# A decoder layer on one core: the order of the work rewritten on all five engines

## The chip, the core and the metric

The kernel runs on one core of one Trainium2 chip. A core has five engines, each with a queue of its own which it works off strictly in order: TensorE (PE; its weight loads are PEld), VectorE (DVE), ScalarE (ACT), GpSimd (POOL) and SyncE (SP), which here only issues transfers. Engines wait for one another through semaphores. The metric is the device time of one execution in microseconds (us), as the median of several runs.

## The reference

x is 16 batches of 128 tokens of 256 values, float32. Three sublayers, each behind a layer norm without weights and added to x:

```python
x = x + attn(norm(x))   # 16 heads over 72 shared latent values, causal softmax
x = x + birwkv(norm(x), ctx, ctx, w, u)
x = x + moe(norm(x))    # 8 experts, top-2 gates, silu(x Wg) * (x Wu) Wd
# attn:   kv = xn @ latent_w + b;  q_h = xn @ Wd_w[h] + b_h
#         y_h = softmax(causal(q_h kv^T / 4)) kv;  out = concat(y_h) @ out_w
# birwkv: ek = exp(ctx); forward and backward scans with decay exp(w) of
#         ek*ctx and of ek; sum of both over sum of both, times sigmoid(xn)
```

## The kernel before

Every piece of work is a step with a name and numbers. `STEPS` (line 109) is one list of all steps, from which the counts are made that semaphores are waited for. What an engine really does in which order stands in a table of its own: `SYNC_STEPS` (198), `TENSOR_STEPS` (210), `VECTOR_STEPS` (232), `SCALAR_STEPS` (261) and `GPSIMD_STEPS` (284). The same name in two tables is the part that each engine has in it. An engine stops at the first step whose wait isn't met, and all behind it stops with it.

The batches stand in four groups of four (g) and eight pairs (k). The steps that matter here:

- Loads, on SyncE: `xl.g` x of group g, `ctx.g` its context (512 KB each), `ow` the output weights (1152 KB), `owh` the same weights by head for the last batch (also 1152 KB), `out.g.*` and `xd.g.*` stores of x and of the normalised x, `lw.j.k` and `ltk.j` weights and token lists of expert tile j.
- Norms: `bn`, `agg` (DVE), `rs` (POOL), `nmb` (DVE), `xn` (ACT), `tx` transposes (PE, then ACT and DVE copy).
- Attention: `q.k.i` is part i of five of the queries of pair k: PE multiplies, ACT copies with bias (line 1142), SyncE moves it by head (lines 713 and 717). There are 64 units n of four heads of one batch: `S.n` scores (PE, line 905), row maxima (DVE, 1373), exponentials (ACT, 1148), `N.n` reciprocal (DVE) and weighing (POOL, 1779), `T.n` transpose (PE, 913) and copy (ACT, 1153), `Y.n` times the values (PE, 923), copy (DVE, 1389) and, for a pair of batches together, packing by three transfers (SyncE, 730 and 731). The copy `Y.n` reuses one of two buffers and waits until the packing of an earlier unit has landed. `O.b.i` is a quarter of the output product of batch b (PE, 946), `xb.i` the bias (POOL, 1786), `add.i` the sum (DVE, 1396).
- Context: `w1` to `w8`, `wa`, `wb` by group and half: `w1` is ek (ACT, 1161) and ek times context (DVE, 1403), `w2` to `w5` are the scans (DVE, 1413 and 1415), `w6`, `w7`, `wa` sums on POOL, `w8` reciprocals (DVE, 1420). The first `w1` also waits for the decay table which POOL builds (line 1762 to 1768).
- Experts: 23 tiles j; the first 16 have 256 rows, the last seven 128. `lxg.j` gathers rows (POOL, 1836; two instructions for a large tile), `tg.j` transposes them, `sw.j.k` splits weights in two (ACT 1213, DVE 1299), `up`, `si`, `hd`, `sh` the hidden layer, `dn.j` the second product (PE) and its weighing into one of two buffers Y (ACT, 1242), `ao.j` adds them to the output by an accumulating indirect transfer (POOL, 1872; two instructions for a large tile). `ao.j` waits until `ao.j-1` has landed, unless both tiles are of one expert, and weighing j waits until `ao.j-2` has landed.

The wait of `ao.j`, in code:

```python
if j > PHASES[0]:
    owed = e.value_load(turns[...], ...)      # 16 or 32 if same expert
    e.wait_ge(s_acc[1 - j % 2], 16 * parts_alike(j - 1) + owed)
elif j:
    po.wait_ge(s_acc[1 - j % 2], 16 * parts_alike(j + 1))
```

Of the kernel before, what the change touches and what calls it, by code (L numbers as in the profile page):

```python
# [96 lines left out]
def gathered(j):  # L97
# [105 lines left out]
    lw.2.2 out.3.0.2 lw.3.1 ltk.4 xd.3.0.2 xd.3.2.2 lw.3.0 out.3.2.2 lw.4.0 lw.4.1 lw.5.1 lw.5.0 ltk.5 lw.6.1 ltk.6 ltk.7 lw.3.2 lw.4.2 ltk.8 ltk.9  # L203
    ltk.10 ltk.11 lw.6.0 ltk.12 lw.7.0 lw.7.1 ltk.13 ltk.14 lw.5.2 ltk.15 ltk.16 lw.8.0 lw.8.1 lw.9.0 lw.9.1 lw.6.2 lw.7.2 lw.10.0 lw.10.1 lw.11.0
    lw.11.1 lw.8.2 lw.9.2 lw.10.2 ltk.17 lw.12.0 ltk.18 ltk.19 ltk.20 lw.13.0 lw.12.1 lw.13.1 ltk.21 lw.14.0 ltk.22 lw.11.2 lw.15.0 lw.14.1 lw.12.2
    lw.13.2 lw.15.1 lw.17.0 lw.14.2 lw.16.0 lw.15.2 lw.17.1 lw.16.1 lw.16.2 lw.18.1 lw.18.0 lw.17.2 lw.19.1 lw.19.0 lw.20.0 lw.21.0 lw.20.1 lw.18.2
# [6 lines left out]
    T.7 Y.6 S.11 S.12 O.0.0 O.0.1 Y.7 T.8 q.2.4 Y.8 O.0.2 T.9 S.13 T.10 Y.9 q.3.0 T.11 va.1 Y.10 O.0.3 S.14 T.12 S.15 O.1.0 O.1.1 O.1.2 q.3.1 Y.11
    wb.0.1 q.3.2 S.16 S.17 T.13 Y.12 T.14 q.3.3 Y.13 wb.1.0 S.18 S.19 O.1.3 T.15 T.16 Y.14 O.2.0 O.2.1 q.3.4 tx.1.2.0.4.0 Y.15 T.17 S.20 S.21
    tx.1.2.0.4.1 O.2.2 Y.16 T.18 O.2.3 Y.17 S.22 S.23 O.3.0 O.3.1 T.19 O.3.2 O.3.3 q.4.0 S.24 kt.2 q.4.1 Y.18 T.20 Y.19 q.4.2 T.21 Y.20 q.4.3 T.22
    S.25 S.26 q.4.4 O.4.0 Y.21 T.23 wb.1.1 O.4.1 Y.22 T.24 S.27 S.28 T.25 Y.23 O.4.2 va.2 Y.24 S.29 S.30 q.5.0 T.26 Y.25 T.27 O.4.3 wb.2.0 Y.26 S.31
# [1754 lines left out]
```

## Time and profile before

| | |
|---|---|
| median of 3 runs | 547.34 us (546.92 to 547.79) |
| profiled execution, its own time | 550.32 us |
| its span, first to last instruction | 548.7 us |
| busy share of the span | PE 91%, PEld 80%, DVE 68%, ACT 61%, POOL 57% |
| mean granted TensorE clock | 0.965 |
| moved by DMA | 76.86 MB, 140 GB/s |

The span is 1.6 us shorter than that execution's own time, which in turn is 3.0 us above the median. Times in the rows are counted from the span's start. A busy time is what the profile has recorded of the instructions; idle time before an instruction is put down to whatever released it. An engine's share over the whole span hides that stages differ: start-up, attention (up to about 300 us), the hand-over to the experts (to about 392 us), the experts, and the end.

### The profile page before, as it was taken

To read this page: it belongs to the slowest core of one execution; us is meant where nothing else is said; L and a number is where in the kernel's file an instruction comes from. 1 tells how busy PE (TensorE), PEld (TensorE's weight loads), DVE (VectorE), ACT (ScalarE), POOL (GpSimd) and SP (SyncE) were. 2 spreads that over 40 slices of the span, in tenths; PEclk is the share of its full clock that TensorE was granted. 3 is DMA by queue.
4 is the path that set the end of the run, shared out by engine and by line. 5 is a ranking of instruction groups with operands and counts; after the bars stand their busy time and mean duration, and the time that the engine had idled before them with its cause. 6 is when DMAs were issued, how large, how long until landed. Compare 5 with 4: busy or idle time off the path is not lost.

```text
span 548.7 us, 10874 instructions
## 1 busy us (share of the span) xinstructions
...
## 2 busy tenths in 40 slices
...
GB/s 233 168 125 100 26 108 117 37 22 163 49 110 95 49 40 55 132 52 67 68 139 44 146 209 214 260 84 215 214 235 244 208 234 237 247 258 276 310 11 0
DMA packets 48087, 76.86 MB, mean 140 GB/s; under 512 B 11053, under 2 KB 29742, under 8 KB 47830
## 3 DMA queue, kind: packets, MB, share of 16 engines
...
## 4 chain that ended last, share of the span: by engine, by line
PE 45%; DVE 16%; issue 12%; DMA 10%; POOL 7%; ACT 4%; POOLq 2%; SPq 1%; another core or an unknown queue 1%; ACTq 0%; DVEq 0%
PE P L830 14%; DMA out<-Y,TK 10%; PE P L905 7%; PE P L923 7%; PE PO L946 7%; PE P L913 4%; PE PO L830 3%; POOL cxa L1836 3%; DVE EB L1373 2%; POOL out L1872 2%; DVE arena L1413 2%; DVE arena L1415 1%; PE P L856 1%; DVE ZT L1389 1%; DVE WF L1299 1%
## 5 line engine op out<-in xcount | busy, mean ns | idle before, releaser
L1779 POOL TENSOR_TENSOR EB<-EB,small 128x512 f32<-128x512 f32 x64 | 72.1, 1138 | 72.9 <-DVE small L1378 72.8
L1148 ACT ACTIVATE EB<-EB,small 128x128 f32<-128x128 f32 x256 | 99.1, 394 | 14.5 <-DVE small L1373 14.5
L830 PE MATMUL P<-GT,WF 128*128 128x256 f32 x768 | 100.4, 291 | 4.2 <-DVE HF L1646 2.0
L1872 POOL DMA_INDIRECT out<-Y,TK x39 | 67.1, 1721 | 61.0 <-DMA out<-Y,TK 32.1
L830 PEld LDWEIGHTS P<-GT,WF 128*128 128x128 f32 x768 | 97.1, 198 | 5.6 <-issue 4.3
L905 PEld LDWEIGHTS P<-KT,qT 72*128 72x128 f32 x512 | 64.9, 198 | 11.2 <-issue 5.6
L905 PE MATMUL P<-KT,qT 72*128 72x128 f32 x512 | 67.5, 282 | 3.2 <-DVE small L1373 3.2
L923 PE MATMUL P<-PT,V 128*72 128x512 f32 x128 | 67.5, 609 | 3.2 <-DVE ZT L1389 2.8
L1153 ACT ACTIVATE PT<-P 128x512 f32<-128x512 f32 x64 | 37.8, 591 | 52.2 <-PE P L913 43.6
L946 PE MATMUL PO<-Ow,zP 128*128 128x256 f32 x270 | 65.6, 384 | 0.9 <-DVE X L1396 0.9
L1373 DVE CUSTOM_DVE_ANT_0 EB<-P,later 128x128 f32<-128x128 f32 x256 | 57.9, 283 | 10.7 <-PE P L913 8.9
L1836 POOL DMA_INDIRECT cxa<-xd,TK x39 | 44.0, 1128 | 27.9 <-DMA TK<-xs 17.0
L946 PEld LDWEIGHTS PO<-Ow,zP 128*128 128x128 f32 x270 | 49.7, 192 | 12.1 <-issue 5.5
L1389 DVE COPY ZT<-P 72x512 f32<-72x512 f32 x64 | 43.3, 676 | 20.2 <-PE P L923 19.4
L830 PE MATMUL PO<-WF,HR 128*128 128x256 f32 x384 | 48.9, 284 | 1.0 <-DVE WF L1299 1.0
L1148 ACT ACTIVATION_READ_ACCUMULATOR EB<-EB,small 128x1 f32 x256 | 49.4, 193 | 0.0
L830 PEld LDWEIGHTS PO<-WF,HR 128*128 128x128 f32 x384 | 47.0, 192 | 1.2 <-DVE WF L1299 1.2
L913 PEld LDWEIGHTS P<-ident,EB 128*128 128x128 f32 x256 | 30.8, 144 | 20.7 <-issue 14.0
...
L913 PE MATMUL P<-ident,EB 128*128 128x128 f32 x256 | 39.8, 279 | 4.3 <-ACT PT L1153 2.5
L830 PE MATMUL P<-xnTa,Wd 128*128 128x256 f32 x216 | 33.5, 308 | 2.4 <-ACT qP L1142 2.0
L1299 DVE TENSOR_TENSOR WF<-arena,WF 128x1024 fp32r<-128x1024 f32 x24 | 29.1, 1220 | 9.5 <-ACT WF L1213 8.4
...
## 6 DMA issues: line engine op xcount, KB each, us to landing
...
```

Of the source, the lines that this page charges most:

```text
L830: r = e.matmul(o, lt(a), rt_(b), start=start and n == 0, stop=stop and n == 2, skip_group_check=skip)
L905: p = e.matmul(S[:, 128 * j:128 * j + 128], qT[k % 2][:, 4 * hq + j, c:c + 128], KT[g % 2][:, r:r + 128], start=True, stop=True)
L913: p = e.transpose(PTB[:, 128 * j:128 * j + 128], EB[n % 3][:, j, :], ident[:, :])
L923: e.matmul(YB[0:L, :], V[g % 2][:, b % GB, :], PT[n % 2][:, :], start=True, stop=True).then_inc(s_Y, 1)
L946: p = e.matmul(o, zP[b // NB % 2][:, m, 128 * (b % NB):128 * (b % NB) + 128], Ow[:, m, :], start=m == 0, stop=m == NQ - 1)
L1148: e.activation(EB[i][:, j, :], EB[i][:, j, :], ACT.Exp, scale=-1.0, bias=NM[i][:, j:j + 1], accum_out=SM[i][:, j:j + 1]).then_inc(s_exp, 1)
L1153: e.activation(PT[n % 2][:, :], PTB[:, :], ACT.Copy).then_inc(s_pt, 1)
L1373: e.tensor_tensor_reduce(out=EB[i][:, j, :], in0=SB[n % 2][:, 128 * j:128 * j + 128], in1=later[:, :], op0=ALU.add, op1=ALU.min, scale=1.0 ...
L1389: e.tensor_copy(ZT[buf][:, :, c:c + 128], YB[0:L, :].rearrange("p (h t) -> p h t", h=4)).then_inc(s_z, 1)
L1779: e.tensor_tensor(EB[i][:, :, :], EB[i][:, :, :], SM[i].unsqueeze(2).broadcast_to([128, 4, 128]), ALU.mult).then_inc(s_prob, 1)
L1836: e.indirect_dma_start(XG[i][:, a_, :], None, xd[0:(TN * 3 // 4, TN + 1)[phase(j)], :], bass.IndirectOffsetOnAxis(ap=TK[:, j, a_, 0:1].bit ...
L1872: e.indirect_dma_start(outr, bass.IndirectOffsetOnAxis(ap=TK[:, j, a_, 0:1].bitcast(i32), axis=0), Y[j % 2][:, a_, :], None, bounds_check= ...
```

## The change

All five engine tables are replaced. Each holds exactly the same steps as before, in another order; `STEPS`, every function, every tile and every wait stay as they are. Of the tables these lines hold the steps that are spoken of below:

```diff
 SYNC_STEPS = """
-    ctx.0 ow xl.1 q.0.0 q.0.1 q.0.2 q.0.3 q.0.4 q.1.0 q.1.1 xl.2 ctx.1 q.1.2 q.1.3 q.1.4 xl.3 Y.1 Y.3 Y.5 q.2.0 q.2.1 Y.7 q.2.2 q.2.3 Y.9 ctx.2 q.2.4
-    q.3.0 q.3.1 Y.11 Y.13 Y.15 Y.17 q.3.2 q.3.3 q.3.4 q.4.0 q.4.1 ctx.3 Y.19 Y.21 Y.23 q.4.2 q.4.3 q.4.4 Y.25 q.5.0 q.5.1 Y.27 Y.29 xd.0.0.4 q.5.2
-    q.5.3 Y.31 Y.33 Y.35 q.5.4 q.6.0 Y.37 Y.39 Y.40 q.6.1 q.6.2 out.0.0.4 q.6.3 q.6.4 Y.41 Y.42 Y.43 Y.44 Y.45 Y.46 Y.47 Y.48 q.7.0 q.7.1 q.7.2 q.7.3
-    Y.49 xd.1.0.4 q.7.4 Y.50 Y.51 out.1.0.4 Y.52 Y.53 Y.54 Y.55 Y.56 owh out.2.0.4 Y.57 Y.58 Y.59 ltk.3 xd.2.0.4 lw.2.0 lw.1.0 lw.1.1 lw.1.2 lw.2.1
...
+    xl.1 ctx.0 q.0.0 q.0.1 q.0.2 q.0.3 q.0.4 xl.2 ow q.1.0 q.1.1 ctx.1 q.1.2 q.1.3 q.1.4 xl.3 Y.1 Y.3 Y.5 Y.7 q.2.0 q.2.1 q.2.2 q.2.3 q.2.4 Y.9 ctx.2
+    Y.11 Y.13 Y.15 q.3.0 q.3.1 q.3.2 q.3.3 q.3.4 q.4.0 q.4.1 Y.17 Y.19 ctx.3 Y.21 Y.23 Y.25 q.4.2 q.4.3 q.4.4 Y.27 q.5.0 q.5.1 q.5.2 Y.29 xd.0.0.4
+    Y.31 Y.33 q.5.3 q.5.4 q.6.0 Y.35 Y.37 out.0.0.4 q.6.1 q.6.2 Y.39 Y.40 Y.41 Y.42 Y.43 q.6.3 xd.1.0.4 q.6.4 Y.44 Y.45 Y.46 Y.47 Y.48 out.1.0.4 Y.49
+    q.7.0 q.7.1 q.7.2 q.7.3 q.7.4 Y.50 Y.51 Y.52 Y.53 Y.54 owh Y.55 xd.2.0.4 Y.56 Y.57 Y.58 Y.59 out.2.0.4 lw.2.0 lw.1.1 lw.1.0 lw.1.2 out.3.0.2 ltk.3
 TENSOR_STEPS = """
-    tx.1.0.0.2.0 tx.1.0.0.2.1 q.0.0 q.0.1 tx.1.0.2.2.0 q.0.2 tx.1.0.2.2.1 q.0.3 kt.0 va.0 q.0.4 q.1.0 S.0 S.1 S.2 q.1.1 q.1.2 q.1.3 T.0 S.3
...
-    tg.16 up.15.0 up.15.1 dn.14 tg.17 up.16.0 dn.15 tg.18 up.17.0 dn.16 tg.19 up.18.0 tg.20 up.19.0 dn.17 dn.18 tg.21 up.20.0 up.21.0 dn.19 tg.22
-    dn.20 up.22.0 dn.21 dn.22
+    tx.1.0.0.2.0 tx.1.0.0.2.1 q.0.0 q.0.1 q.0.2 q.0.3 tx.1.0.2.2.0 tx.1.0.2.2.1 kt.0 va.0 S.0 S.1 q.0.4 q.1.0 S.2 S.3 q.1.1 q.1.2 tx.1.1.0.4.0 T.0
...
+    up.15.0 up.15.1 dn.14 tg.17 up.16.0 up.17.0 tg.18 dn.15 tg.19 dn.16 tg.20 up.18.0 dn.17 up.19.0 up.20.0 tg.21 dn.18 dn.19 dn.20 tg.22 up.21.0
+    up.22.0 dn.21 dn.22
 VECTOR_STEPS = """
...
-    bn.1.1.0.0 bn.1.1.0.2 agg.1.1.0.4 nmb.1.1.0.4 w1.0.0 w2.0.0 w3.0.0 w4.0.0 S.0 S.1 w5.0.0 S.2 w8.0.0.0 vb.0 N.0 N.1 w8.0.0.1 w8.0.0.2 w8.0.0.3
-    w1.0.1 w2.0.1 w3.0.1 w4.0.1 w5.0.1 Y.0 S.3 N.2 tx.1.1.0.4.0 S.4 N.3 Y.1 tx.1.1.0.4.1 bn.1.2.0.0 bn.1.2.0.2 S.5 N.4 w8.0.1.0 Y.2 agg.1.2.0.4 N.5
...
+    bn.1.1.0.0 bn.1.1.0.2 agg.1.1.0.4 w1.0.0 w2.0.0 w3.0.0 nmb.1.1.0.4 S.0 S.1 w4.0.0 w5.0.0 vb.0 N.0 N.1 S.2 w8.0.0.0 w8.0.0.1 w8.0.0.2 w8.0.0.3 S.3
+    w1.0.1 w2.0.1 N.2 w3.0.1 w4.0.1 w5.0.1 tx.1.1.0.4.0 Y.0 S.4 tx.1.1.0.4.1 N.3 S.5 Y.1 bn.1.2.0.0 N.4 S.6 Y.2 N.5 w8.0.1.0 w8.0.1.1 N.6 w8.0.1.2
 SCALAR_STEPS = """
-    xn.1.0.0.0 tx.1.0.0.2.0 tx.1.0.0.2.1 wq.1 wq.2 xn.1.0.2.0 consts q.0.0 q.0.1 tx.1.0.2.2.0 tx.1.0.2.2.1 kt.0 q.0.2 w1.0.0 q.0.3 q.0.4 w2.0.0 w4.0.0
-    S.0 q.1.0 S.1 w1.0.1 xn.1.1.0.0 xn.1.1.0.2 q.1.1 S.2 w2.0.1 w4.0.1 q.1.2 q.1.3 T.0 tx.1.1.0.4.0 T.1 S.3 tx.1.1.0.4.1 q.1.4 T.2 w1.1.0 S.4 S.5 T.3
...
-    sw.7.2 sw.10.1 sh.7.0 sh.7.1 tg.10 dn.5 sh.8.0 sh.8.1 si.9.0 sw.10.0 si.9.1 sw.8.2 dn.6 sh.9.0 dn.7 sh.9.1 sw.11.0 sw.11.1 tg.11 sw.9.2 sw.10.2
...
-    dn.18 si.19.0 si.20.0 tg.21 tg.22 dn.19 dn.20 si.21.0 si.22.0 dn.21 dn.22
+    xn.1.0.0.0 tx.1.0.0.2.0 tx.1.0.0.2.1 wq.1 wq.2 q.0.0 q.0.1 xn.1.0.2.0 consts q.0.2 tx.1.0.2.2.0 tx.1.0.2.2.1 kt.0 w1.0.0 w2.0.0 w4.0.0 q.0.3 q.0.4
+    S.0 q.1.0 S.1 xn.1.1.0.0 xn.1.1.0.2 q.1.1 w1.0.1 S.2 q.1.2 q.1.3 T.0 S.3 tx.1.1.0.4.0 w2.0.1 w4.0.1 q.1.4 T.1 tx.1.1.0.4.1 w1.1.0 S.4 T.2 S.5 S.6
...
+    si.6.0 sw.7.0 si.6.1 sw.7.1 sw.8.1 sh.5.1 sh.6.0 sh.6.1 sw.5.2 sw.8.0 si.7.0 si.7.1 sw.6.2 tg.8 dn.4 sw.9.1 sh.7.0 dn.5 si.8.0 sw.9.0 sw.7.2 tg.9
...
+    tg.21 dn.17 si.20.0 dn.18 tg.22 dn.19 dn.20 si.21.0 si.22.0 dn.21 dn.22
 GPSIMD_STEPS = """
-    rs.1.0.0.2 rs.1.0.2.2 q.0.0 rs.1.1.0.4 w6.0.0 w7.0.0 N.0 N.1 xb.2 xb.3 wa.0.0 N.2 N.3 xb.0 w6.0.1 w7.0.1 N.4 N.5 N.6 N.7 N.8 wa.0.1 w6.1.0 N.9
...
-    ao.8 ao.9 ao.10 ao.11 lxg.17 lxg.18 lxg.19 ao.12 ao.13 lxg.20 ao.14 ao.15 lxg.21 ao.16 lxg.22 ao.17 ao.18 ao.19 ao.20 ao.21 ao.22
+    rs.1.0.0.2 rs.1.0.2.2 q.0.0 rs.1.1.0.4 w6.0.0 w7.0.0 N.0 xb.2 N.1 N.2 wa.0.0 xb.3 N.3 w6.0.1 w7.0.1 N.4 N.5 N.6 wa.0.1 N.7 w6.1.0 N.8 w7.1.0 N.9
...
+    ao.7 ao.8 ao.9 lxg.16 ao.10 ao.11 ao.12 lxg.17 lxg.18 lxg.19 lxg.20 ao.13 ao.14 ao.15 lxg.21 ao.16 lxg.22 ao.17 ao.18 ao.19 ao.20 ao.21 ao.22
```

There are two buffers Y for weighted results before and after.

## Rows read from the trace of the kernel before

**Rows 1.** Busy us by stretch and engine; then TensorE clock, DMA share, GB/s.

```profile
0.00:60.00 60.00, 46.26 (x306) 39.68 (x307) 42.04 (x134) 36.53 (x110) 35.47 (x50) 0.94 0.53 148
60.00:300.00 240.00, 233.81 (x1478) 191.05 (x1477) 185.67 (x784) 170.85 (x620) 138.25 (x120) 0.98 0.32 77
300.00:392.00 92.00, 78.42 (x510) 69.00 (x509) 67.76 (x189) 50.05 (x91) 56.30 (x54) 0.94 0.66 189
392.00:512.00 120.00, 119.32 (x995) 118.27 (x994) 73.51 (x91) 73.22 (x122) 71.47 (x48) 1.00 0.88 244
512.00:549.00 37.00, 23.81 (x152) 21.96 (x151) 2.66 (x4) 5.45 (x12) 11.88 (x8) 0.84 0.24 78
```

**Rows 2.** The same view, stretches of ten microseconds.

```profile
30.00:40.00 10.00, 9.40 (x68) 8.84 (x67) 10.00 (x19) 9.82 (x31) 8.86 (x7) 0.89 0.46 135
...
270.00:280.00 10.00, 8.59 (x58) 6.44 (x56) 7.61 (x38) 7.97 (x28) 5.04 (x5) 1.00 0.52 139
280.00:290.00 10.00, 9.70 (x53) 8.29 (x52) 6.57 (x41) 6.07 (x27) 7.07 (x8) 0.74 0.41 109
```

**Rows 3.** SyncE's queue in order of time, start-up; columns start, us.

```profile
7.49 0.56 SPq L697 DMA_DIRECT2D cxa<-ctxin  x1
...
9.97 0.43 SPq L678 DMA_DIRECT2D X<-x  x1
```

**Rows 4.** VectorE in order of time, start-up; brackets: idle before, its releaser.

```profile
20.32 1.40 DVE L1334 BATCH_NORM_STATS2 small<-X 128x6 f32<-128x256 f32 x4 [3.85 <-DMA X<-x]
...
23.58 0.69 DVE L1403 TENSOR_TENSOR arena<-cxa,arena 128x512 f32<-128x512 f32 x1
24.18 1.23 DVE L1415 TENSOR_TENSOR_SCAN arena<-D,arena 128x517 f32<-128x517 f32 x1
...
38.29 2.26 DVE L1413 TENSOR_TENSOR_SCAN arena<-D,arena 128x517 f32<-128x517 f32 x1
```

**Rows 5.** GpSimd in order of time, start-up.

```profile
19.47 0.11 POOL L1768 MEMSET D<- 128x5 f32 x1
...
35.48 3.98 POOL L1786 TENSOR_TENSOR X<-X,small 128x512 f32<-128x512 f32 x2
```

**Rows 6.** TensorE in order of time, start-up.

```profile
23.35 1.95 PE L905 MATMUL P<-KT,qT 72*128 72x128 f32 x16
...
28.54 1.91 PE L905 MATMUL P<-KT,qT 72*128 72x128 f32 x8 [3.25 <-DVE small L1373]
```

**Rows 7.** SyncE's queue, parts of the last pair's queries.

```profile
258.92 12.15 SPq L717 DMA_DIRECT2D qT<-qP  x6
```

**Rows 8.** VectorE and TensorE in order of time, around 308 us.

```profile
308.29 0.69 DVE L1396 TENSOR_TENSOR X<-PO,X 128x512 f32<-128x512 f32 x1 [3.21 <-remote]
...
309.04 1.13 PE L946 MATMUL PO<-Ow,zP 128*128 128x256 f32 x4 [0.91 <-DVE X L1396]
```

**Rows 9.** GpSimd in order of time, expert stage and end.

```profile
427.58 1.95 POOL L1872 DMA_INDIRECT out<-Y,TK  x1 [4.04 <-ACT Y L1242]
...
480.33 1.01 POOL L1836 DMA_INDIRECT cxa<-xd,TK  x1 [0.30 <-issue]
...
490.57 1.55 POOL L1872 DMA_INDIRECT out<-Y,TK  x1 [0.30 <-issue]
...
499.06 1.58 POOL L1872 DMA_INDIRECT out<-Y,TK  x1 [3.77 <-DMA out<-Y,TK]
...
531.21 1.55 POOL L1872 DMA_INDIRECT out<-Y,TK  x1 [4.23 <-ACT Y L1242]
...
539.64 1.55 POOL L1872 DMA_INDIRECT out<-Y,TK  x1 [0.30 <-issue]
```

**Rows 10.** The chain of waits, end; columns start, us.

```profile
525.43 3.67 DMA out<-Y,TK
```

**Rows 11.** ScalarE and TensorE in order of time, end.

```profile
520.64 0.47 ACT L1242 ACTIVATE Y<-PO,TK 128x256 f32<-128x256 f32 x1 [5.98 <-DMA out<-Y,TK]
...
522.58 5.44 PE L1022 MATMUL P<-GS,WS 128*128 128x128 f32 x32 [2.92 <-ACT GS L1219]
```

More of the change, by code:

```diff
@@ L203 @@
[L203 to L206, printed above, removed]
@@ new lines @@
+    q.7.0 q.7.1 q.7.2 q.7.3 q.7.4 Y.50 Y.51 Y.52 Y.53 Y.54 owh Y.55 xd.2.0.4 Y.56 Y.57 Y.58 Y.59 out.2.0.4 lw.2.0 lw.1.1 lw.1.0 lw.1.2 out.3.0.2 ltk.3
+    ltk.4 lw.2.1 lw.3.1 lw.3.0 out.3.2.2 lw.2.2 xd.3.0.2 xd.3.2.2 lw.4.0 lw.4.1 lw.5.0 lw.5.1 ltk.5 lw.3.2 ltk.6 ltk.7 ltk.8 lw.6.0 ltk.9 ltk.10
+    lw.6.1 ltk.11 lw.4.2 ltk.12 ltk.13 ltk.14 lw.7.0 lw.7.1 lw.8.1 lw.5.2 lw.6.2 ltk.15 ltk.16 ltk.17 lw.8.0 lw.9.0 lw.9.1 lw.10.0 lw.7.2 lw.10.1
+    lw.8.2 lw.9.2 lw.11.0 lw.11.1 lw.10.2 lw.12.0 ltk.18 ltk.19 lw.12.1 lw.13.1 ltk.20 ltk.21 lw.13.0 lw.11.2 lw.14.1 lw.12.2 lw.14.0 lw.15.0 lw.15.1
@@ L208 @@
+    lw.13.2 lw.17.1 lw.17.0 lw.16.0 lw.14.2 lw.16.1 ltk.22 lw.18.0 lw.15.2 lw.18.1 lw.16.2 lw.17.2 lw.19.1 lw.20.1 lw.19.0 lw.18.2 lw.20.0 lw.21.1
+    lw.22.1 lw.21.0 lw.19.2 lw.22.0 lw.20.2 lw.21.2 lw.22.2
 """
 TENSOR_STEPS = """
-    tx.1.0.0.2.0 tx.1.0.0.2.1 q.0.0 q.0.1 tx.1.0.2.2.0 q.0.2 tx.1.0.2.2.1 q.0.3 kt.0 va.0 q.0.4 q.1.0 S.0 S.1 S.2 q.1.1 q.1.2 q.1.3 T.0 S.3
-    tx.1.1.0.4.0 q.1.4 Y.0 S.4 T.1 tx.1.1.0.4.1 Y.1 T.2 S.5 T.3 kt.1 Y.2 q.2.0 S.6 S.7 Y.3 wb.0.0 T.4 T.5 S.8 q.2.1 Y.4 S.9 S.10 q.2.2 Y.5 T.6 q.2.3
@@ L213 @@
[L213 to L216, printed above, removed]
@@ L230 @@
+    up.10.0 dn.8 up.10.1 up.11.0 up.11.1 tg.12 dn.9 tg.13 up.12.0 up.12.1 tg.14 dn.10 dn.11 up.13.0 up.13.1 tg.15 dn.12 up.14.0 up.14.1 dn.13 tg.16
+    up.15.0 up.15.1 dn.14 tg.17 up.16.0 up.17.0 tg.18 dn.15 tg.19 dn.16 tg.20 up.18.0 dn.17 up.19.0 up.20.0 tg.21 dn.18 dn.19 dn.20 tg.22 up.21.0
+    up.22.0 dn.21 dn.22
 """
 VECTOR_STEPS = """
-    bn.1.0.0.0 agg.1.0.0.2 nmb.1.0.0.2 split bn.1.0.2.0 agg.1.0.2.2 tx.1.0.0.2.0 tx.1.0.0.2.1 wq.1 nmb.1.0.2.2 wq.2 tx.1.0.2.2.0 tx.1.0.2.2.1
-    bn.1.1.0.0 bn.1.1.0.2 agg.1.1.0.4 nmb.1.1.0.4 w1.0.0 w2.0.0 w3.0.0 w4.0.0 S.0 S.1 w5.0.0 S.2 w8.0.0.0 vb.0 N.0 N.1 w8.0.0.1 w8.0.0.2 w8.0.0.3
```

120 lines of the change are left out of this document (62 added, 58 removed).

## The prediction

> **What bounds the kernel now.** I read the busy time by stretch first [rows 1]. TensorE is the bound, and unevenly. In the first 60 us it is busy 46.26, so 13.7 are idle; from 60 to 300 us only 6.2 of 240 are; in the hand-over 13.6 of 92; from 392 to 512 us 0.7 of 120; in the last 37 us 13.2. A new order removes no work, so it can win only in the idle time, 47 us in all, and where the clock is granted at half speed (1.2 instead of 2.4 GHz): 0.94 in the first and third stretch, 0.84 in the last.
>
> Then the timelines of single engines in those stretches. At the start VectorE sets the pace: from 30 to 40 us it is busy 10.00 of 10.00 [rows 2], after it had waited 3.85 us for x of group 1 [rows 4]. That transfer was issued at 9.97, behind the context (issued 7.49) and the 1152 KB of output weights [rows 3], and landed at 20.3. TensorE meanwhile idles 3.25 us for VectorE's row maxima [rows 6].
>
> At the end a second chain takes over, the additions to the output. Each waits for the one before to land, as at 499.06 (3.77 us of waiting for a transfer) [rows 9]. ScalarE stands 5.98 us before the weighing of tile 18, which needs tile 16's addition landed, and TensorE 2.92 us behind the copy `tg.21` that is queued behind this weighing [rows 11].
>
> **Start-up: -2.9 us.** x of group 1 now takes the context's place in the queue, so it is issued at about 7.5 instead of 9.97 with 1664 KB fewer before it. If its landing takes even 9 of the 10.3 us that it took, it is there at 16.5, when VectorE has done what stands before, and the norm statistics (1.40) [rows 4] run in its former idle time. The context lands later by one 512 KB transfer, but its first use on ScalarE can't come before the decay table is ready, at 19.6 [rows 5]. ek, on ScalarE, has the size of VectorE's product (0.69) [rows 4]; with 0.6 for it `w1.0.0` can start at 20.2 instead of 23.58: 3.4 us earlier. From there to the row maxima of unit 4 its old and its new list hold the same steps; only `nmb`, `S.3`, `tx` and `N.2` change places. VectorE had no idle time there, so all 3.4 us arrive if none arises. The new order has places where some may: `S.2` and `S.3` now wait for queries that ScalarE copies behind `w4`, and `w8` for GpSimd. I take off 0.5. `S.0` and `S.1` ahead of `q.0.4` and `q.1.0` on TensorE are needed for this: their scores stood at 23.35 behind both [rows 6], and need only query parts 0 and 1. Past 60 us TensorE is full, so the lead stays.
>
> What could eat it is GpSimd. A scan takes 1.23 us with GpSimd idle and 2.26 beside its bias addition [rows 4], which itself takes 1.99 [rows 5]. Before, three scans met such an instruction. The new list has `N.2`, `wa` and `xb.3` beside `w3` to `w5` of the second half, three again, if `xb.2` and `N.1` have finished before. Every further meeting costs 1.03. With three more the gain is nil; with one or two fewer the term is -4.2. So the bounds are 0.2 and -4.2.
>
> The Trainium skill ("SBUF — State Buffer", Who interferes with whom) makes this an exclusive lock: of a VectorE instruction with two SBUF inputs and a GpSimd one that reads SBUF, the later waits for the earlier's whole length. By that rule a meeting costs VectorE up to a GpSimd instruction, not a fixed 1.03, and three more of them could turn the start-up into a loss of about 2.6 (3 x 1.99 - 3.4); the row of 2.26 against 1.23 agrees with an added wait, and no row shows a longer one.
>
> `xl.2` moves ahead of `q.1`, and `ow` behind it, to about 25 us. Both are hidden: by the lists x of group 2 is read after `Y.1` and the output weights after `S.10`, and even the 10.3 us that x of group 1 took to land end by 37, when unit 4 isn't reached. If these 1664 KB delay the moves of `q.1`, the cost is 0 to 2 us, since `S.8` is the first to need them; I take 0.
>
> **The middle of attention: 0, bounds +7.8 and -6.** Summed over each engine's list, the work ahead of `S.n`, `N.n` and `Y.n` differs between the two orders by -7 to +5 us, with both signs and no drift. With 6.2 us idle out of 240 there is little to win. What can be lost shows at 258.92, where SyncE stood 12.15 us on the parts of the last pair's queries with a packing behind them [rows 7]; soon after, TensorE was idle for 1.4 of the 10 us from 270, and the next ten ran at a clock of 0.74, which is 2.5 us lost on 9.70 busy [rows 2]. One such event costs 3.9. The new SyncE list takes `Y.49` out of that place, and puts `Y.17` behind `q.4.0` and `q.4.1`, `Y.35` behind `q.5.4` and `q.6.0`, `Y.39` behind `q.6.1` and `q.6.2`. Behind a late packing stands VectorE's next copy into the same buffer, behind that its row maxima, and TensorE waits for these. One event less and none new would be -3.9; two new ones +7.8.
>
> **The hand-over: -1.0, bounds +1 and -3.** VectorE stood 3.21 us before adding batches 12 and 13 and TensorE 0.91 for that sum [rows 8], just after SyncE had issued `owh` and `out.2`, 1664 KB, ahead of the packing of units 57 to 59. Now `owh` goes two units earlier and `out.2` last. I take TensorE's 0.9 us and, with the copies of units 59 and 60 behind VectorE, round to 1.0; all of VectorE's stand would be 3. On the other side, `Y.55` and `xd.2` now stand behind `owh`; `O.13.3`, which needs `Y.55`, comes only after `Y.57`, two units on. If that isn't enough it costs 1. The rest of the 13.6 idle us (norms of group 3, choice, plan, token lists) keeps its order; `ltk.3` and `ltk.4` move, but have until `tg.3` and `tg.4`, behind all of tiles 0 and 1's `up`.
>
> **The end: -1.1, bounds +4 and -4.** Three edits. First, ScalarE weighs tile 5 right behind its product instead of behind `tg.10`: `ao.5`, which waited 4.04 us for it and started at 427.58 [rows 9], can start some 5 us sooner, as tile 4's addition has landed. From there to `ao.12` the chain goes from landing to landing and keeps that lead. Second, the gathers 17 to 20 now stand between `ao.12` and `ao.13`. Before, 17 to 19 began at 480.33 in the wait for a landing and cost nothing; now the four, one instruction of 1.31 us each (1.01 and 0.30) [rows 9], cost 5.2 us. `ao.13`, at 490.57 with no wait, thus starts about where it did: +0.2. Third, on ScalarE `si.19`, `tg.21` and `si.20` pass the weighing of tile 18, so TensorE has tile 21's rows in time. But `dn.20`, which needs that weighing, now stands before `up.21` and `up.22`. What is left to win is the wait of `ao.19` for its Y: it started at 531.21 after 4.23 us of waiting [rows 9], and tile 18's addition, issued at 525.43, took 3.67 to land [rows 10]. Landed at 529.1 and 0.8 to react, my estimate for one round of waiting, it could have gone at 529.9: 1.3 sooner. The last addition, at 539.64, comes earlier by these 1.3. Sum -1.1. If `tg.17` finds its rows late as well, up to +4; if the lead of 5 us isn't paid back, -4.
>
> **Sum.** -2.9 + 0 - 1.0 - 1.1 = -5.0: the profiled execution would be 545.3 instead of 550.32, the span 543.7. Its own time is 3.0 above the median; taken off the median of 547.34, that is 542.3 us.
>
> **Rivals.**
> - The additions to the output are the bound and the gathers in their way cost 3 more than reckoned (the lead of 5 us lost to landings, which slow under the load of the weights): -2.9 - 1.0 + 3.2 = -0.7, 546.6. For it: ScalarE's 5.98 and GpSimd's 3.77 are both waits for these transfers. Against it: `ao.5` waited for ScalarE, not for a landing. 15%.
> - Slower: the packings behind queries. Two events of 3.9 in the middle against -3.9 from the start-up and hand-over, and the end unchanged: +3.9, 551.2. It decides where SyncE comes to `Y.17` or `Y.35` more than about 4 us (a unit) after VectorE's copy. For it: SyncE's wait at 258.92. Against it: the old list had `Y.11` to `Y.17` behind `q.3.0` and `q.3.1` without a dip in the clock there. 14%.
> - The lead of the start-up is given back to three more scans that meet GpSimd: -1.0 - 1.1, 545.2. 8%.
> - More is won: the dip at 280 to 290 and the idle time before it go as well: -8.9, 538.4. 13%.
> - The new order does nothing at all: hardly possible, since VectorE waits for the very transfer that moves. In the first rival.
>
> **How the numbers follow.** My forecast has 50%; its own range is 540 to 545.5. What this kernel's measurement can tell from no change is about 0.2%, 1.1 us (546.2 to 548.4). Faster: 45 of my 50, 5 of the 15, 7 of the 8, all 13: 0.70. Slower: 14, and 3 more of the others: 0.17. The rest, 0.13, is the same. The range for 8 in 10 leaves out the ends of the slower and of the best case: 537.8 to 549.
>
> **What would show it.** Right: VectorE's wait for x in the first 25 us gone and its first product with the context near 20; the first 60 us with 3 us more TensorE work done; `ao.5` near 420; the wait of TensorE near 520 gone from behind `tg.21`. Wrong: a first product still near 23; new idle time of TensorE behind VectorE's copies of units 20 or 38; `ao.13` later than its turn by more than 5 us, or a granted clock below 0.96.

## Result, and the profile after the change

The changed kernel takes 541.28 us (median of 4 runs, 538.61 to 543.16), the kernel before 547.13 (4 runs beside it): ratio 0.989 (95% interval 0.985 to 0.994), 5.9 us faster. In the later series it was run again beside the kernel before: 541.42 against 546.47, ratio 0.990 (0.986 to 0.993). Medians and ranges are of all runs of a kernel; ratios are formed from its fast runs alone, those within 1.5% of its fastest. The profiled execution took 542.01 us, its span is 540.4.

The same five stretches as [rows 1], after the change (the last one ends with the span):

```profile
0.00:60.00 60.00, 50.44 (x327) 43.75 (x328) 43.74 (x142) 40.19 (x124) 36.97 (x52) 0.91 0.55 148
60.00:300.00 240.00, 234.82 (x1500) 190.84 (x1498) 193.57 (x817) 170.91 (x615) 146.79 (x128) 1.00 0.36 85
300.00:392.00 92.00, 81.69 (x578) 75.68 (x579) 67.32 (x159) 56.50 (x96) 55.01 (x50) 0.94 0.68 192
392.00:512.00 120.00, 114.56 (x927) 113.22 (x926) 65.84 (x80) 63.60 (x107) 64.43 (x44) 0.97 0.85 241
512.00:540.00 28.00, 16.52 (x107) 14.61 (x105) 1.97 (x3) 4.96 (x11) 9.34 (x6) 0.86 0.14 33
```

TensorE gains 4.2 busy us in the first 60, though part of them at the slow clock (0.91 against 0.94). From 392 to 512 us it loses 4.8 busy us and some of its clock: 114.56 at 0.97 where it was 119.32 at 1.00. That stretch had nothing to win, and it lost. (The windows stand at fixed times, and the work in them is shifted by the lead; the table below compares at equal work.)

At the start, VectorE no longer waits for x of group 1 [rows 4]; the statistics follow the copies at 17.09. VectorE after the change, in order of time:

```profile
16.41 0.76 DVE L1299 TENSOR_TENSOR xnTa<-P,xnTa 128x256 fp32r<-128x256 f32 x2 [2.75 <-ACT xnTa L1124]
17.09 1.39 DVE L1334 BATCH_NORM_STATS2 small<-X 128x6 f32<-128x256 f32 x4
...
20.96 0.69 DVE L1403 TENSOR_TENSOR arena<-cxa,arena 128x512 f32<-128x512 f32 x1 [1.86 <-ACT arena L1161]
21.57 1.23 DVE L1415 TENSOR_TENSOR_SCAN arena<-D,arena 128x517 f32<-128x517 f32 x1
...
25.58 1.96 DVE L1415 TENSOR_TENSOR_SCAN arena<-D,arena 128x517 f32<-128x517 f32 x1
...
36.12 1.20 DVE L1413 TENSOR_TENSOR_SCAN arena<-D,arena 128x517 f32<-128x517 f32 x1
37.24 2.00 DVE L1415 TENSOR_TENSOR_SCAN arena<-D,arena 128x517 f32<-128x517 f32 x1
39.16 2.23 DVE L1413 TENSOR_TENSOR_SCAN arena<-D,arena 128x517 f32<-128x517 f32 x1
```

The first product with the context starts at 20.96, 2.6 us earlier than before. ScalarE's step ahead of it, and what that waited for:

```profile
20.30 0.63 ACT L1161 ACTIVATE arena<-cxa 128x512 f32<-128x512 f32 x1 [0.75 <-POOL D L1768]
```

The additions to the output that answer to [rows 9] (tile 5, then 12 with the gathers and 13, then 16, 19 and 22), GpSimd in order of time:

```profile
410.95 2.67 POOL L1872 DMA_INDIRECT out<-Y,TK  x1 [0.30 <-issue]
...
475.76 1.56 POOL L1872 DMA_INDIRECT out<-Y,TK  x1 [7.01 <-ACT Y L1242]
477.62 1.56 POOL L1872 DMA_INDIRECT out<-Y,TK  x1 [0.30 <-issue]
479.48 1.02 POOL L1836 DMA_INDIRECT cxa<-xd,TK  x1 [0.30 <-DMA out<-Y,TK]
480.81 1.04 POOL L1836 DMA_INDIRECT cxa<-xd,TK  x1 [0.30 <-issue]
482.16 0.95 POOL L1836 DMA_INDIRECT cxa<-xd,TK  x1 [0.31 <-issue]
483.41 0.95 POOL L1836 DMA_INDIRECT cxa<-xd,TK  x1 [0.30 <-issue]
484.66 2.09 POOL L1872 DMA_INDIRECT out<-Y,TK  x1 [0.30 <-issue]
...
509.06 1.58 POOL L1872 DMA_INDIRECT out<-Y,TK  x1 [5.96 <-DMA out<-Y,TK]
...
525.49 1.55 POOL L1872 DMA_INDIRECT out<-Y,TK  x1 [3.56 <-ACT Y L1242]
...
531.30 1.55 POOL L1872 DMA_INDIRECT out<-Y,TK  x1 [0.30 <-issue]
```

Tile 5's addition comes 16.6 us earlier than before, tile 13's only 5.9, the last one 8.3. Much was won up to 411 us, and 10.7 us of it were given back by 485.

SyncE's stand on the last pair's queries [rows 7], and the tens of us of [rows 2], after the change:

```profile
262.34 6.18 SPq L717 DMA_DIRECT2D qT<-qP  x8
```
```profile
270.00:280.00 10.00, 9.46 (x68) 7.80 (x69) 6.08 (x37) 6.09 (x16) 6.71 (x7) 1.00 0.27 61
280.00:290.00 10.00, 9.84 (x68) 7.95 (x67) 9.07 (x60) 7.12 (x33) 7.05 (x8) 1.00 0.71 158
```

At the end, TensorE's wait of 2.92 us behind the copy of tile 21's rows [rows 11] is gone; 0.83 for a weighing is left (TensorE in order of time):

```profile
516.34 1.97 PE L1031 MATMUL PO<-WS,HS 128*128 128x256 f32 x8 [0.83 <-ACT Y L1242]
518.14 0.38 PE L988 MATMUL P<-ident,cxa 128*128 128x128 f32 x2
518.36 7.31 PE L1022 MATMUL P<-GS,WS 128*128 128x128 f32 x64
```

To see where the lead is won and lost, I compare TensorE's work. For each stretch of 5 us in the view by stretch I multiply TensorE's busy time by its granted clock and sum up; the table gives the difference in the time at which two executions reach the same sum (minus: earlier than the profiled execution of the kernel before, whose own times stand in the second column). The columns: the changed kernel, the changed kernel again, and of the experiments below p3 (old order behind the hand-over), t1 (one edit on ScalarE in the changed kernel), p2 (new order for start and attention), s1 (transfers alone), p4 (new expert stage and end alone).

```
work   before   after  again    p3     t1     p2     s1     p4
 60     77.4    -2.6   -3.3   -6.4   -6.2   -4.9   -1.0   +1.2
100    118.6    -2.7   -3.4   -6.5   -6.4   -5.0   -1.0   +1.2
180    202.1    -5.9   -6.6   -9.7   -9.6   -8.2   -2.6   -0.4
240    262.3    -6.0   -6.7   -9.8   -9.7   -8.3   -2.6   -0.4
280    309.1   -10.2  -10.5  -14.2  -14.0   -7.2   -6.4   -3.3
340    384.0   -12.1  -10.9  -14.5  -15.3   -7.0   -8.1   -2.1
360    405.1   -11.8  -11.5  -14.9  -16.0   -6.5   -2.9   +4.2
380    425.1    -8.0   -7.9  -14.3  -14.5   -6.2   -2.7   +4.4
420    465.8    -7.7   -6.1  -14.8  -13.3   -5.6   -2.1   +5.3
440    485.8    -3.9   -1.8  -14.3  -13.3   -5.3   -1.5  +10.1
460    505.8    -3.9   -1.8  -14.3  -11.6   -5.3   -1.5  +10.1
480    530.1    -7.3   -5.8  -14.3  -15.7   -5.2   -1.8   +6.6
```

The changed kernel loses 3.6 to 3.8 us of its lead between 360 and 380 of work, and 3.8 to 4.3 between 420 and 440, in both its profiles. In p3, which differs from it only behind the hand-over, the lead stays between 14 and 15 us from 340 to the end. At the end the new order wins 3.4 to 4.1 (from 460 to 480, in the columns after, again, t1 and p4).

Not each loss in the table is an order's. Between 340 and 360 s1 loses 5.2 and p4 6.3. s1 has the old expert order there, and so has p1, whose profile loses 3.7 in the same place. In all three TensorE stood before the second product of an early tile (2.35 us at 388.26 in s1, 3.42 at 388.91 in p1, 4.66 at 390.74 in p4; 1.01 at 391.56 in the kernel before, where it waited for split weights). So p4's drop there can't be put down to the new order. Its drop between 420 and 440, 4.8 us, stands where the changed kernel and its repeat lose too.

### The profile page after: what moved, and what is told of

Same layout as the page of the kernel before. It is cut to its first block, busy times and chain, and to the rows that moved or that the text cites. A ratio compares the mean times of both kernels' runs of the same rounds, so it can differ in the third digit from the quotient of the medians.

```text
span 540.4 us, 10872 instructions
## 1 busy us (share of the span) xinstructions
PE 498.0 (92%) x3432; PEld 438.1 (81%) x3432; DVE 372.4 (69%) x1199; ACT 336.2 (62%) x949; POOL 312.5 (58%) x278
## 4 chain that ended last, share of the span: by engine, by line
PE 42%; DMA 13%; POOL 13%; DVE 13%; issue 12%; ACT 2%; POOLq 2%; SPq 1%; DVEq 0%; ACTq 0%
PE P L830 12%; DMA out<-Y,TK 11%; PE P L923 7%; PE PO L946 7%; PE P L905 7%; PE P L913 4%; POOL xs L1822 3%; POOL out L1872 3%; POOL cxa L1836 3%; DVE EB L1373 2%; PE PO L830 2%; POOL EB L1779 2%; DVE arena L1413 2%; DVE arena L1415 2%; DMA cxa<-xd,TK 1%
## 5 line engine op out<-in xcount | busy, mean ns | idle before, releaser
L1779 POOL TENSOR_TENSOR EB<-EB,small 128x512 f32<-128x512 f32 x64 | 74.3, 1170 | 72.3 <-DVE small L1378 72.2
L830 PE MATMUL P<-GT,WF 128*128 128x256 f32 x768 | 101.5, 293 | 5.0 <-DVE HF L1646 3.7
L830 PEld LDWEIGHTS P<-GT,WF 128*128 128x128 f32 x768 | 98.3, 201 | 6.1 <-issue 4.4
L1822 POOL DMA_INDIRECT xs<-TKS,SL x32 | 32.5, 1016 | 22.6 <-DVE TKS L1509 14.6
L1227 ACT ACTIVATE SG<-P 128x512 f32<-128x512 f32 x39 | 22.9, 596 | 26.8 <-PE P L830 17.8
L1142 ACT ACTIVATE qP<-P,small 128x256 f32<-128x256 f32 x72 | 30.1, 464 | 12.8 <-PE P L830 11.9
```

The lines of the kernel that those rows point to most:

```text
L830: r = e.matmul(o, lt(a), rt_(b), start=start and n == 0, stop=stop and n == 2, skip_group_check=skip)
L1779: e.tensor_tensor(EB[i][:, :, :], EB[i][:, :, :], SM[i].unsqueeze(2).broadcast_to([128, 4, 128]), ALU.mult).then_inc(s_prob, 1)
L1822: e.indirect_dma_start(xs, bass.IndirectOffsetOnAxis(ap=SL[:, g, c, b:b + 1], axis=0), TKS[:, g, c, b, :], None).then_inc(s_sc[g], 16)
```

## Experiments

All are permutations of the step lists, so none leaves work out. Every table is cut at places where the old and the new list have done the same steps (the start-up's cut differs by a step or two on three engines); "new" and "old" below are the lists of the changed kernel and of the kernel before. Ratios are to the kernel before in the same series; its median was 551.55, 546.47 and 547.75 us in the three series, so times of different series are not subtracted, only ratios. The profiled executions of p1_start, p4_experts, x1_best, x2_old_transfers and x3_both_mended were among the longer ones of their kernels, so of these I use waits, marks, and losses between two points of work, not the whole lead.

### First series: which stage brings it

**p1_start.** New order on all engines up to about unit 8, old behind.

```diff
 SYNC    new up to Y.5  | old from q.2.0
 TENSOR  new up to S.10 | old from T.6
 VECTOR  new up to S.10 | SCALAR new up to w4.1.0 | GPSIMD new up to w6.1.0
```

> The new order on all five engines for the start-up alone (VectorE up to the row maxima of unit 10, TensorE up to their scores), the old order behind it. Theory: the start-up brings the 2.7 us that the trace of the changed kernel shows as TensorE's lead at 100 us, and nothing behind it gives them back: about 544.4 us against 547.1 (ratio 0.995). Rival: the lead is lost again behind later stages that have limits of their own (landings of the additions, arrival of expert weights), so 546.5 to 547.1 (0.999 to 1.000).

Measured: 545.83 us (12 runs), ratio 0.988 (0.984 to 0.992). The start-up brings 1.2% of 551.55, 6.8 us (4.7 to 8.9; the medians of all runs differ by 5.7), about twice what the theory (2.7) and my prediction (2.9) had, and nothing behind it gives it back in time. The rival is refuted.

**s1_transfers.** SyncE's queue alone.

```diff
-    ctx.0 ow xl.1 q.0.0 q.0.1 q.0.2 q.0.3 q.0.4 q.1.0
+    xl.1 ctx.0 q.0.0 q.0.1 q.0.2 q.0.3 q.0.4 ow q.1.0
```

> The kernel before with two transfers moved in SyncE's queue and nothing else: x of group 1 ahead of the context, the output weights behind the first queries. Theory: these transfers are the whole cause of the start-up's gain, since VectorE's wait of 3.85 us for x goes with them: 544.4 to 545.2 us. Rival: without the scores of units 0 and 1 ahead of the fifth query part on TensorE the lead isn't passed on, and the context lands too late for its first user: 546.5 to 548 us.

Measured: 550.63 us (12 runs), ratio 0.9975 (0.993 to 1.002). Not told from nothing; the interval holds the theory (0.995 to 0.997) as well as the rival (0.999 and more). But it is clearly less than p1's gain (the intervals don't touch). The transfers alone aren't the start-up's gain. Yet its VectorE reaches the first product nearly as early as in the changed kernel:

```profile
21.33 0.69 DVE L1403 TENSOR_TENSOR arena<-cxa,arena 128x512 f32<-128x512 f32 x1
```

A mark that the granted clock disturbs little is the start of the transposes of group 1's x, for which TensorE waits on VectorE. TensorE in order of time, in before, after, s1 and p4 (old start-up), one fence each:

```profile
45.97 1.11 PE L856 MATMUL P<-ident,XN 128*128 128x128 f32 x4 [3.89 <-DVE xnTb L1299]
```
```profile
42.03 1.11 PE L856 MATMUL P<-ident,XN 128*128 128x128 f32 x4 [2.91 <-DVE xnTb L1299]
```
```profile
43.72 1.12 PE L856 MATMUL P<-ident,XN 128*128 128x128 f32 x4 [3.90 <-DVE xnTb L1299]
```
```profile
47.52 0.92 PE L856 MATMUL P<-ident,XN 128*128 128x128 f32 x4 [3.86 <-DVE xnTb L1299]
```

From the first product to this mark VectorE needs 22.4 us in before and in s1, 21.1 after the change. So the transfers bring 2.3 us here and the new order 1.7 more. What the order brings on VectorE's way can be named. In the old start-up four scans run longer than the 1.2 us of a scan alone, in before, s1 and p4 by the same amounts; VectorE in order of time, before:

```profile
29.25 1.74 DVE L1413 TENSOR_TENSOR_SCAN arena<-D,arena 128x517 f32<-128x517 f32 x1
...
36.06 2.31 DVE L1415 TENSOR_TENSOR_SCAN arena<-D,arena 128x517 f32<-128x517 f32 x1
```

and then 2.26 at 38.29 and 2.23 at 40.48. In the changed kernel there are three (1.96, 2.00 and 2.23, shown above), so 1.1 us less are lost beside GpSimd. The copy `Y.0` (0.66) now stands behind the mark, and the product `w1.0.1` takes 1.00 where it took 0.62. The old start-up has a second face: in p4 VectorE stood 5.57 us before x instead of 3.85, and the mark is 1.6 us later than in the profile on which I predicted.

**p2_attention.** New order for start and attention, old from the hand-over on (SyncE from `Y.55`, TensorE from `O.12.2`, VectorE from `p2.0`, ScalarE from `T.61`, GpSimd from `gtk.0`).

> The new order for start-up and attention up to the packing of unit 54, the old order from the hand-over on (expert stage and end as before). Theory: TensorE is 9 to 11 us ahead at 290 us of the changed kernel's trace, and it is the new order of the expert stage that gives most of it back: with the old one about 537 to 539 us (ratio 0.984). Rival: the expert stage is held by weights and additions whatever its order, so that a TensorE that comes early only waits there: 541 to 543 us, the changed kernel's time or more.

Measured: 543.9 us (6 runs), ratio 0.988 (0.982 to 0.994). That is nearer to the rival (0.989 and more) than to the theory (0.984), and the interval holds both. Compared with p1's 0.988 the middle adds nothing that this measurement sees. Its lead at the end, 5.2 us, is where the start-up left it (5.0 at 100); it had 8.2 at 180 and lost 1.1 at the dip in the clock described below.

**p4_experts.** Old order up to the hand-over's end, new for expert stage and end.

> The old order up to the first addition to the output, the new order for expert stage and end. Theory: between 355 and 430 us the new order loses by itself 5 to 9 us of TensorE's time (idle, and the clock after it), and the end brings 3.4: 549 to 553 us. Rival: the loss there comes only from TensorE's being early, so at the old pace nothing is lost and the end's gain is left: 543.7 us.

Measured: 555.1 us (12 runs), ratio 1.0046 (1.0006 to 1.0086). Slower by 2.5 us (0.3 to 4.7), as the theory had it: the new expert order costs by itself, also when TensorE comes late. The rival, 3.4 us faster, is refuted.

### Second series: where the gain is given back

**after_again.** The changed kernel.

> The changed kernel once more, beside the other versions of this series: ratio 0.989 to the kernel before, as at first. All theories expect this; a ratio above 0.995 would mean that its gain depends on the chip or the moment.

Measured: 541.42 us (12 runs), ratio 0.990 (0.986 to 0.993). As at first.

**p3_to_handover.** New up to the last scatters of the token lists, old for expert stage and end.

```diff
 SYNC    new up to the stores of group 3 | old from lw.4.0
 TENSOR  new up to lg.3.0.4.2    | old from up.0.1
 VECTOR  new up to rw.3.0.4      | SCALAR new up to sw.4.1 | old from dn.0
 GPSIMD  new up to r4.3.0.4.1.2  | old from ao.0
```

> The new order up to the last scatter of the token lists, the old one for expert stage and end. Theory: the new expert order loses 4 to 8 us by itself and the new end wins 3.4, so this one is 1 to 4 us faster than the whole change (ratio 0.983 to 0.987). Rival: the expert stage is bound by weights and additions and gives back whatever TensorE brings: the ratio stays 0.989 or rises by the end's 3.4 us to 0.995.

Measured: 534.54 us (6 runs, 533.76 to 536.12), ratio 0.979 (0.974 to 0.983). 6 us less than the changed kernel in the same series, with intervals that don't touch, and more than the theory had (0.983 to 0.987). The expert stage gives nothing back if its old order stays; the rival falls.

**p5_old_experts.** As p3, but new from tile 12 on (SyncE from `ltk.18`, TensorE from `up.13.0`, VectorE from `hd.12.0`, ScalarE from `sw.15.1`, GpSimd from `ao.11` on).

> The changed kernel with the old order for the middle of the expert stage only (tiles 2 to 11), and the new one at the end. Theory: the losses of the changed kernel at 400 to 410 and 450 to 470 us go (4.8 and 3.8 us of work in its trace) and the end's 3.4 stay won: 6 to 8 us less than the whole change, ratio about 0.976. Rival: the landings of the additions pace the stage, TensorE's idle time only moves: the changed kernel's 0.989.

Measured: 539.57 us (6 runs, 536.31 to 547.01), ratio 0.986 (0.980 to 0.991). The theory fails: the end isn't won on top. Its TensorE stood 2.04 us for weights at 441.57 and 2.94 for tile rows at 462.97, around the place where the lists are joined. Both times ScalarE had stood for a weight transfer, 3.14 us at 438.07 and 2.51 at 459.36, and at the second VectorE's part of the row copy was queued behind its wait for ScalarE. That is another wait than the changed kernel's in the same place (below), and I have no run that tells the joint's own cost from the new order's. The end's win was there again in TensorE's work, 4.0 us from 460 to 480.

**t1_weigh_behind_copy.** The changed kernel with one edit on ScalarE.

```diff
-    sh.12.0 sw.12.2 dn.10 dn.11 si.13.0 sh.12.1 sw.13.2 tg.14 si.13.1
+    sh.12.0 sw.12.2 si.13.0 sh.12.1 sw.13.2 tg.14 dn.10 dn.11 si.13.1
```

> The changed kernel with one edit on ScalarE: the weighings of tiles 10 and 11 come behind the copy of tile 14's rows, as in the kernel before. Theory: TensorE's 2.35 us without work before tile 15's transposes (ScalarE waits 3.11 us for a landing with that copy queued behind) and the slower clock behind it go, 3.8 us: ratio 0.982. Rival: the additions are the bound there, and a later weighing delays them, so nothing is won: 0.989 to 0.990.

In the changed kernel, ScalarE weighs tile 11 only when tile 9's addition has landed, and the copy of tile 14's rows stands behind that and three more steps:

```profile
456.36 0.82 ACT L1242 ACTIVATE Y<-PO,TK 128x256 f32<-128x256 f32 x2
460.29 0.84 ACT L1242 ACTIVATE Y<-PO,TK 128x256 f32<-128x256 f32 x2 [3.11 <-DMA out<-Y,TK]
461.02 0.60 ACT L1227 ACTIVATE SG<-P 128x512 f32<-128x512 f32 x1
461.49 0.64 ACT L1234 ACTIVATE HR<-HF 128x512 fp32r<-128x512 f32 x1
462.01 1.06 ACT L1213 ACTIVATE WF<-WR 128x1024 fp32r<-128x1024 f32 x1
462.96 0.60 ACT L1221 ACTIVATE GT<-P 128x512 fp32r<-128x512 f32 x1
```

VectorE makes the second part of the copy, out of ScalarE's, and TensorE waits for that. It pays 2.35 us and then a clock of 0.83 over the ten us from 460 (VectorE, then TensorE in order of time, then the view by stretch):

```profile
463.60 0.69 DVE L1299 TENSOR_TENSOR GT<-P,GT 128x512 fp32r<-128x512 f32 x1 [0.66 <-ACT GT L1221]
```

```profile
464.43 1.09 PE L988 MATMUL P<-ident,cxa 128*128 128x128 f32 x4 [2.35 <-DVE GT L1299]
```
```profile
460.00:470.00 10.00, 7.65 (x54) 7.47 (x53) 6.75 (x9) 7.29 (x12) 6.85 (x4) 0.83 0.87 235
```

The same pair of waits stands in the changed kernel's repeat (ScalarE 3.57 us for the landing, TensorE 2.83 at 465.72) and in p4 (4.37, and 3.48 at 481.25). With the edit, the copy (455.00) runs ahead of both weighings (455.48, four of them) and the stretch is full:

```profile
455.00 0.59 ACT L1221 ACTIVATE GT<-P 128x512 fp32r<-128x512 f32 x1
455.48 1.57 ACT L1242 ACTIVATE Y<-PO,TK 128x256 f32<-128x256 f32 x4
```
```profile
460.00:470.00 10.00, 10.00 (x86) 10.00 (x85) 5.83 (x8) 3.72 (x8) 4.48 (x3) 1.00 0.77 188
```

Measured: 537.93 us (6 runs), ratio 0.986 (0.981 to 0.991). The mechanism is shown: in the table t1 loses nothing from 420 to 440 where the changed kernel loses 4. (It loses 1.2 just before, from 380 to 420, where TensorE stands 1.77 us at 448.45 ahead of tile 11's last product, and 1.7 behind, for gathered rows.) In time it is 3.5 us less than the changed kernel by the medians of this series and 2.0 by the ratios, where the theory had 3.8; the intervals of the two ratios overlap, so the size is not shown.

### Third series: the start-up's parts, and better versions

**x2_old_transfers.** p3 with `ctx.0 ow xl.1` at the head of SyncE's queue.

> The version with the new order up to the hand-over and the old one behind it (ratio 0.9785), with the three transfers at the head of SyncE's queue back in their old order: context, output weights, x of group 1. Theory of the prediction: the moved transfer is the start-up's whole gain, so 2.9 us are lost (ratio 0.984) and TensorE's lead at 100 us of work shrinks to 1 to 2 us. Rival, from the traces so far: the order of the steps on the engines is worth more than the transfer (the transfers alone gave 1.6 us, all of the new start-up 4 to 5): the loss is 1.5 us or less.

Measured: 540.67 us (6 runs), ratio 0.988 (0.984 to 0.992), against p3's 0.979 with intervals that don't touch: 5.4 us lost, where the theory had 2.9 and the rival 1.5 or less. The rival falls; the new order needs the transfers. VectorE stood 4.29 us for x again, and the mark of the transposes came at 47.91 instead of 41.80. Only 2.4 of these 6.1 us are the later first product (23.14 against 20.72): on the way to the mark VectorE stood twice more, 1.83 us for ScalarE's exponentials at 33.11 and 1.92 for TensorE at 39.32. Without the transfers the new order thus takes longer to the mark than the old one, 24.8 us against 22.4. This fits that the transfers are worth little alone and much under the new order.

**x4_scores_late.** p3 with one edit on TensorE.

```diff
-    kt.0 va.0 S.0 S.1 q.0.4 q.1.0 S.2 S.3
+    kt.0 va.0 q.0.4 q.1.0 S.0 S.1 S.2 S.3
```

> The same version (ratio 0.9785) with one edit on TensorE: the scores of units 0 and 1 stand behind the fifth part of the first and the first part of the second pair's queries again, as in the kernel before. Theory of the prediction: VectorE's row maxima of unit 0 then wait for their scores, and part of the lead goes, 0.5 to 2 us (ratio 0.9795 to 0.982). Rival: the scores are ready early enough either way, nothing is lost.

Measured: 536.09 us (6 runs), ratio 0.980 (0.976 to 0.985). Against 0.979 that can't be told apart in time. In the trace the step is right: the mark comes at 44.39 against 41.80 in p3, with the first product only 0.5 later (21.20 against 20.72). VectorE stood 2.00 and 0.67 us for its scores; 2.1 us of its chain are lost.

**x1_best.** p3 with the new tail on TensorE from `up.16.0` and on ScalarE from `tg.17` on.

> The new order up to the hand-over, the old expert order, and the new order on TensorE and ScalarE alone from tile 16's products on (the old one otherwise, the gathers 17 to 19 before tile 12's addition too). Theory: the new tail takes 3.4 us of TensorE's time in the last 60 us away (its wait of 3.02 behind tile 21's copy goes), and with it the last addition comes earlier: ratio 0.973 where the version without this tail had 0.9785. Rival: the additions end the kernel whatever TensorE does, one landing after another: ratio 0.9785 or more.

Measured: 535.72 us (6 runs), ratio 0.977 (0.973 to 0.982). Best ratio of all, but not told from p3, nor from the theory's 0.973. So what the new tail brings in time is not shown. From tile 16's addition to the last it took 22.9 us, against 25.2 in p3, 26.1 before and 22.2 in the changed kernel.

**x3_both_mended.** t1 and a second edit: in the changed kernel ScalarE stood 3.06 us at 398.82 for weights of tile 8, with tile 8's rows and tile 4's weighing queued behind.

```diff
 SCALAR
-    sw.5.2 sw.8.0 si.7.0 si.7.1 sw.6.2 tg.8 dn.4
+    sw.5.2 si.7.0 si.7.1 sw.6.2 tg.8 dn.4 sw.8.0
 VECTOR
-    sw.5.2 sw.8.0 tg.8
+    sw.5.2 tg.8 sw.8.0
```

> The changed kernel with two places of the expert stage mended: the weighings of tiles 10 and 11 behind the copy of tile 14's rows on ScalarE (0.9858 alone), and the split of tile 8's first weight part behind tile 8's rows on ScalarE and VectorE, where ScalarE waits 3.06 us for that part. Theory: TensorE's wait before tile 9's rows and the slower clock behind it (3.75 us lost at 400 to 410) go too: ratio 0.979. Rival: TensorE then waits for the weights of tile 8 themselves, and nothing is won beyond 0.9858.

Measured: 539.57 us (6 runs), ratio 0.984 (0.980 to 0.989), not told from t1's 0.986. The theory (0.979) fails, and the rival is right in that nothing more is won, though not in what TensorE waits for. Its wait before tile 9's rows (0.93 at 403.15 in the changed kernel, and 1.12 more at 404.91) is gone, and one for VectorE's gated products stands in its place, of 2.20 at 406.88: as much in sum. From 360 to 380 of work this version loses 3.5 us as before. So the cause of that loss isn't this one step. That it lies in the expert order is shown by p3; which step of it is to blame stays open.

## Why the prediction was right, and where its terms were not

Forecast 542.3, measured 541.28: the sum was right. Its terms were not; their errors cancelled, and that is luck. p3 measures all that stands ahead of the experts: 11.7 us won (9.4 to 14.0) where my three terms for it add up to 3.9. Expert stage and end cost about 6 where I had 1.1 won.

**Start-up, -2.9.** The mechanism is right at most points that I named. The wait for x is gone, the first product starts at 20.96 (I had 20.2: ScalarE waited 0.75 for GpSimd's decay table, which was ready at 20.2 and not 19.6), and three scans ran longer beside a GpSimd instruction: 1.96, 2.00, 2.23 where 1.20 is a scan alone. The Trainium skill ("SBUF — State Buffer", Who interferes with whom) would allow a wait of a whole GpSimd instruction; the longest seen adds 1.1 (2.31 in the kernel before, beside additions of 1.99 each), so no row goes against it. What I had wrong is the count before: not three but four, with the one of 1.74 at 29.25. And one meeting fewer is -3.9 by my own price, not the -4.2 of my bound. The size of the term is wrong: 6.8 us (4.7 to 8.9, p1). The failed step is the one that begins "From there to the row maxima of unit 4 its old and its new list hold the same steps", with the 3.4 us that "arrive if none arises" and the 0.5 taken off: I priced the order at a small loss, and it is a gain. Of the 3.9 us gained at the mark of the transposes 2.6 are the earlier product and 1.3 the order on VectorE's way from there, 1.1 of them the shorter scans; x4 shows that `S.0` and `S.1` behind the query parts would cost 2.1 us of VectorE's chain, so they were needed for it, as predicted. The rest may be the base, which is not shown: [rows 4] show one execution of the old start-up, and p4's shows one in which x came 1.6 us later. In the nine profiles with the whole new start-up TensorE reaches 60 of work 1.5 to 6.4 us earlier than in before, 4.2 on average, and 1.2 later in p4. Against the mean of these two that makes 4.8 us, at the low end of p1's interval.

**Middle, 0.** Right by p1 and p2 (0.988 both). In the traces the work from 100 to 180 is reached with 3.2 us more lead in each execution of the new order, 1.6 in s1, p4 and p1 with the old one and 0 in the profile that I read, since that one had a dip of the clock at 182 to 186 us of its own. So the order may be worth 1.6 us; the times don't resolve it. The dip at 280 to 290 us [rows 2], which I priced at 3.9 as SyncE's doing, isn't tied to SyncE's stand, which shrank from 12.15 [rows 7] to 6.18 us. With the old order and its stand of 12.12 us s1 had no dip (1.00 from 280 to 300, where before had 0.74 and 0.92), and p4, with 12.15, a shorter one (0.84 and 0.99). The other way round p2 has the short stand and a clock of 0.66 from 275 to 285. The rival of two new packing waits didn't come about.

**Hand-over, -1.0.** TensorE's named wait went: its 0.91 us for the sum of batches 12 and 13 [rows 8] are gone in the changed kernel, its repeat and p3. VectorE still stands before that sum, 2.53 us instead of 3.21, but now for TensorE's product. With the old hand-over TensorE still stood for that sum, 0.75 in p1 and 1.40 in p2. From 280 to 340 of work the lead grows by 0.3 to 1.9 in the columns after, again, p3 and t1 and shrinks by 0.2 in p2. That looks like my 1.0, but with the old hand-over it grows by 1.7 in s1 and shrinks by 1.2 in p4, so the traces don't show the term. From p2 to p3 the ratio falls by 0.010, 5.3 us, over two series and with intervals that just overlap. What of that is the hand-over's stays open, since p2's profile also has the dip above; it is the largest piece of the gain that no run explains.

**End, -1.1.** Wrong in sign, and the largest error. The three edits did what I worked out: tile 5's addition came earlier, by 16.6 us, of which 8 to 12 are TensorE's lead at that work, which leaves 5 to 9 for the order (I had 5); four gathers cost tile 13's addition 4.0 us (8.90 from tile 12's to tile 13's start, 4.86 before; I had 5.2); and from tile 16's addition to the last 22.2 us pass instead of 26.1, 3.9 won where I had 1.3. I had it at tile 19's wait, which gave 0.6; 2.6 came behind that, where tile 21's addition had waited 3.17 us for its weighing (at 537.78) and now waits 0.55. What I left out is the stretch between. I read 0.7 us idle of 120 [rows 1] as a stretch in which nothing happens. But a full stretch is one in which a new order can only lose. ScalarE's list now has weighings, each of which waits for a landing, ahead of copies that TensorE needs. The price of expert stage and end together is +2.5 (0.3 to 4.7) at the old pace and, as the difference of the changed kernel to p3, +6.

The additions-bound rival (546.6) was wrong as a bound: with p3 TensorE keeps its whole lead to the end. Its idea, waits for landings, was right, on ScalarE in place of GpSimd. The time of 538.4 that I gave to "more is won" would have been passed but for this stage: p3 runs at 0.979 of the kernel before, 535.6 on my median of 547.34.
